# A new order of tasks in an attention and feed-forward kernel, half-array masks, and a cast on GpSimd

## The chip, the cores and the metric

The kernel runs on one core of one Trainium2 chip. The metric is the device time in microseconds (us) of one execution. The engines are TensorE (PE in the profile, its weight loads PEld), VectorE (DVE), ScalarE (ACT), GpSimd (POOL) and SyncE (SP), which only issues DMAs. Each works through its own queue in order, and they meet at semaphores.

## What is computed

For eight sequences of 1024 tokens with 256 channels the reference does, cut to what matters:

```python
xn = layernorm(x)
q, k, v = split(xn @ W_attn + b_attn)            # 16 heads of 16
q, k = rope(q), rope(k)       # its position index runs over the heads' axis
att = where(causal, q @ k.T / sqrt(16), -inf)
s = softmax(att) @ v @ W_proj + b_proj
g = silu((silu(xn @ Wg.T) * (xn @ Wu.T)) @ Wd.T) # hidden size 768, int weights / 127
out = x + s * g
```

## The kernel before

**Batches, units, slots.** The work is cut into 8 batches. A batch has 4 units, each of 4 heads, and a unit has 12 steps: a step is one block of keys (128) against one chunk of queries (512). `BLOCKS` lists the steps, and `width(n)` is the number of queries that step n needs: 512, 384, 256, 128 for the first chunk, and five times 512, then 384, 256, 128 for the second. So a batch has 48 slots, numbered 0 to 47, and slot s is step s mod 12 of unit s div 12. `body` runs over the slots, the first batch as "first", the last as "last", the six between as "mid".

**A slot on TensorE.** It has two halves. Each half begins with two score matmuls (`scores`, L672), which write keys by queries into a ring of three banks `st`. Each uses one half of the array's rows: 48 rows of split q and k and 2 rows that subtract the row maximum. Then come matmuls of the maxima (`maxima`, L696): q by k once more for the unit that is 16 slots ahead, also in pairs on the two halves of the rows, written into the ring of four banks `ring`. The maxima of the first half of a slot are on the diagonal, so a mask is added there: a matmul of `tri` with `identb` (L704) per bank, with all 128 rows. After that the first half has the slot's tasks, and the second half has the values (L722), the products of the exponentials of the step before with v, in four column strips. The second half has maxima in 8 of 12 slots.

**The other engines.** ScalarE takes the exponential of each score bank (`exps`, L896), two a half, and copies or activates the results of the tasks in the order of the table. VectorE reduces each bank of the maxima (L1030) and does its parts of the tasks. GpSimd sets the masked part of the exponentials to zero with an affine select (`mask`, L1250) at the start of a slot whose step before was on the diagonal (steps 0 to 3 and 8 to 11), then its parts of the tasks. SyncE stores q and k to a scratch in HBM, loads them back as stacks (`load_stack`, L508), six DMAs for q and six for k per unit, and loads and stores x.

**Tasks.** `TASKS` names, for each slot, the tasks of its first half; `END_TASKS` replaces it in the last batch from a slot on. The names: LNS (layer norm statistics, VectorE), LNR (the chain for the reciprocal deviation, 14 small operations on GpSimd, L470 to L478), LNA (normalise one tile, GpSimd), TX (transpose of xn), QK and V (projections), XC (a copy of the second half of the tokens, GpSimd), UPG and UPU (gate and up products of one of six chunks of 128 hidden units), DN (down product of 128 tokens), YT (transpose of the attention's result, read by VectorE), FT and FP (transpose and projection of the output), MT (transpose of the maxima, copied by ScalarE at L964). FP of one batch, its last two DN and one YT are done in the next. LNS, LNR, LNA, TX and QK are for the next batch.

`LAG` says how many half slots after the task's slot an engine does its part. The feed-forward chunk goes UPG: ScalarE tanh, VectorE `ga`; UPU: ScalarE copy `ups`, GpSimd product `hf` (L1281); then HI on ScalarE: `hT` high part, the 16-bit rounding of `hf` (L915); then LO on GpSimd: `hT` low part, the difference (L1286).

**Before the first slot.** `prologue` prepares weights, the first batch's norm, q, k and v, and then does the maxima of the first 16 steps, which VectorE has to reduce. SyncE loads the q stacks of units 0 and 1, ScalarE issues the 12 DMAs of their k stacks ahead of its copies of the last four QK.

Of the kernel before, what the change touches and what calls it, by code (L numbers as in the profile page):

```python
# [26 lines left out]
BLOCKS = [(0, k) for k in range(4)] + [(1, k) for k in range(8)]  # L27
# [27 lines left out]
def full_item(s):  # L55
# [18 lines left out]
    12: [("UPG", 0, 3), ("UPU", 0, 3), ("XC", 1)],
    13: [("YT", 0, 0), ("UPG", 0, 4), ("LNA", 0)],
    14: [("UPU", 0, 4)],
    15: [("FT", 2), ("FT", 3)],
    16: [("UPG", 0, 5), ("UPU", 0, 5), ("LNA", 2)],
    17: [("YT", 0, 1), ("LNA", 6)],
    18: [("YT", 1, 0), ("LNA", 3)],  # L80
    19: [("LNA", 1)],
    20: [("TX", 1, 0), ("DN", 0, 0), ("LNA", 4), ("LNA", 5), ("LNA", 7)],
    21: [("MT", 2), ("TX", 1, 1)],
    22: [("TX", 0, 1), ("DN", 0, 1)],
    23: [("QK", 0, 0, 1), ("QK", 0, 1, 1)],
# [17 lines left out]
    41: [("YT", 2, 1), ("UPU", 1, 5)],
    42: [("YT", 3, 0), ("QK", 1, 0, 0)],
    44: [("QK", 1, 1, 1)],
    45: [("MT", 0)],
# [11 lines left out]
EPI = [("YT", 3, 1), ("FT", 2), ("FT", 3), ("FP", 2), ("FP", 3)]  # L118
END_TASKS = {
    29: [("UPG", 1, 0)],  # L120
    30: [("DN", 0, 3)],
    31: [("UPU", 1, 0)],
    32: [("UPG", 1, 1)],
    33: [("MT", 3), ("UPG", 1, 2), ("UPU", 1, 1)],
    34: [("UPU", 1, 2)],
    35: [("UPG", 1, 3), ("UPU", 1, 3)],
    36: [("YT", 1, 1), ("UPG", 1, 4), ("UPU", 1, 4)],
    37: [("YT", 2, 0), ("UPG", 1, 5), ("UPU", 1, 5)],
    41: [("YT", 2, 1), ("DN", 1, 0)],
    42: [("YT", 3, 0), ("DN", 1, 1)],  # L130
    43: [("FT", 0, "end"), ("FT", 1, "end"), ("DN", 1, 2, "end")],
    44: [("FP", 0, "end")],
    45: [("DN", 1, 3, "end"), ("FP", 1, "end")],
# [13 lines left out]
def tasks_at(kind, slot):  # L147
    tasks = END_TASKS if kind == "last" and slot >= min(END_TASKS) else TASKS
# [4 lines left out]
def has_max(kind, slot):  # L153
# [152 lines left out]
def build_program(nc, x, w_attn, b_attn, w_proj, b_proj, w_gate_t, w_up_t, w_down_t, rope_cos, rope_sin, out):  # L306
# [8 lines left out]
    with ExitStack() as ctx:  # L315
# [18 lines left out]
        identb = sb("identb", [P, P], bf16)  # L334
# [87 lines left out]
        tri_done = sem("tri_done")  # L422
        pv_done = sem("pv_done")
# [106 lines left out]
        def _(sp):  # L530
# [42 lines left out]
            def task(kind, i, t):  # L573
                if t[0] == "QK":
                    _, hf_, which, c = t
                    if t == [u for u in BY["QK"].seen[kind] if u[1:3] == (hf_, which)][-1]:
                        store_parts(kind, i, hf_, which)
                        if hf_ == 0 and which == 1:
# [4 lines left out]
                if t[0] == "FP":  # L583
                    store_out(kind, i, t)
                    if t[1] < 2:
                        load_xo(own_batch(i, t), t[1] + 2)

            def prologue():
# [11 lines left out]

                sp.wait_ge(b_turned, 1)
# [18 lines left out]
            def body(kind, i):  # L620
                for slot in range(SLOTS):
                    for half in range(2):
# [29 lines left out]
        def _(pe):  # L652
# [22 lines left out]
            def maxima(kind, i, slot, half):  # L675
# [730 lines left out]
```

## Time and profile before

| | us |
|---|---|
| median of 3 runs | 1412.45 |
| lowest, highest | 1411.94, 1413.13 |
| the profiled execution | 1412.94 |
| its span, first to last instruction | 1411.2 |
| mean granted TensorE clock | 0.979 |

A profile shows one execution. Busy time of an engine is the union of its instructions' times; a matmul's time holds its way through the array, so two that overlap in the pipeline count once, and how far apart they start tells more than how long each lasts. The timeline merges instructions of one kind that follow each other and gives the count behind an x; in square brackets it gives the idle time before them and what ended it.

### The profile page before, as it was taken

The numbers are of one execution on the slowest core, as the hardware profiler recorded it, in microseconds if no ns is written. First come the engines' busy times: TensorE is split into PE (matmuls) and PEld (weight loads), VectorE is DVE, ScalarE is ACT, GpSimd is POOL, SyncE is SP. The second block draws the span as 40 slices with busy tenths as digits, with TensorE's granted clock in tenths as the row PEclk, the third lists the DMA queues.
The fourth block names the chain that finished last, engine by engine and source line by source line (L and its number), as shares of the span: only waits on it lengthen the run. The fifth ranks groups of instructions, "written<-read, shape, count | busy, mean of one in ns | idle before, by whom it ended". The sixth has DMA issues, their size and how long they took to land.

```text
span 1411.2 us, 28890 instructions
## 1 busy us (share of the span) xinstructions
PE 1333.2 (94%) x10631; PEld 549.7 (39%) x10631; DVE 1007.6 (71%) x1930; ACT 983.3 (70%) x2186; POOL 626.5 (44%) x751
## 2 busy tenths in 40 slices
PE   3899999999999999999999999999999999999986
PEld 1223433434344433434334343443334443343333
DVE  6688777777777767787777777777777777767711
ACT  2157677786767777676777767777776777778673
POOL 4117332573426444464435734265343643344352
PEclk9679999999999999999999999999999999999998
DMA  2620112202041020401213020410204002120101
GB/s 79 171 76 2 48 30 96 56 1 92 2 120 32 2 91 17 128 10 36 57 53 99 2 79 14 120 33 2 91 16 121 17 10 83 37 85 2 31 2 46
DMA packets 56769, 73.58 MB, mean 52 GB/s; under 512 B 9010, under 2 KB 34994, under 8 KB 56628
## 3 DMA queue, kind: packets, MB, share of 16 engines
q1 hardware_dynamic: 56052, 70.95, 16.7%
q8 instruction: 84, 1.38, 0.4%
q10 hardware_dynamic: 576, 0.79, 0.3%
q14 instruction: 57, 0.47, 0.1%
HBM read 46.01 MB, written 25.17 MB: 50 GB/s over the span
## 4 chain that ended last, share of the span: by engine, by line
PE 71%; ACT 11%; DVE 9%; issue 4%; POOL 3%; DMA 1%; ACTq 0%; POOLq 0%; SPq 0%; DVEq 0%
PE ring L730 24%; PE acc L722 15%; PE st L672 11%; PE ring L696 7%; PE ring L704 5%; ACT pexp L896 4%; PE ring L817 4%; DVE mx_a L1030 3%; ACT th L942 2%; PE ring L792 2%; DVE ga L1092 1%; ACT mT L964 1%; ACT parts L932 1%; PE ring L826 1%; PE ring L807 1%
## 5 line engine op out<-in xcount | busy, mean ns | idle before, releaser
L896 ACT ACTIVATE pexp<-st 128x512 f32<-128x512 f32 (+3 forms) x1536 | 659.4, 494 | 82.5 <-PE st L672 78.6
L1030 DVE TENSOR_REDUCE mx_a<-ring 128x1 f32<-128x512 f32 (+3 forms) x896 | 534.5, 646 | 134.3 <-PE ring L704 74.8
L1250 POOL TENSOR_SCALAR_AFFINE_SELECT pexp<-pexp 128x512 f32<-128x512 f32 x256 | 162.5, 635 | 510.3 <-ACT pexp L896 510.3
L722 PE MATMUL acc<-pexp,v_pad 128*17 128x512 f32 (+3 forms) x3072 | 324.3, 494 | 15.6 <-POOL pexp L1250 12.4
L672 PE MATMUL st<-q_st,k_st 50*128 50x512 f16 (+3 forms) x1536 | 299.8, 335 | 17.6 <-ACT pexp L896 16.1
L696 PE MATMUL ring<-k_st,q_st 48*128 48x512 f16 (+3 forms) x1536 | 270.0, 333 | 9.7 <-DMA k_st<-parts_scratch 6.0
L1030 DVE TENSOR_REDUCE mx_b<-ring 128x1 f32<-128x384 f32 (+3 forms) x384 | 212.8, 596 | 53.2 <-PE ring L704 50.4
L672 PEld LDWEIGHTS st<-q_st,k_st 50*128 50x128 f16 x1536 | 85.0, 93 | 409.1 <-ACT pexp L896 268.3
L1281 POOL TENSOR_TENSOR hf<-ga,ups 128x512 f32<-128x512 f32 x96 | 121.8, 1269 | 68.6 <-ACT ups L947 57.1
L1286 POOL TENSOR_TENSOR hT<-hf,hT 128x512 f16<-128x512 f32 x96 | 111.0, 1157 | 91.3 <-ACT hT L915 91.3
L704 PE MATMUL ring<-tri,identb 128*128 128x128 bf16 (+1 forms) x768 | 126.1, 247 | 0.0
L1092 DVE SCALAR_TENSOR_TENSOR ga<-th,ring 128x512 f32<-128x512 f32 x96 | 66.0, 688 | 57.4 <-ACT th L942 57.2
L722 PEld LDWEIGHTS acc<-pexp,v_pad 128*17 128x17 f32 x3072 | 51.5, 95 | 131.0 <-issue 108.1
L696 PEld LDWEIGHTS ring<-k_st,q_st 48*128 48x128 f16 x1536 | 84.3, 96 | 41.5 <-DVE mx_a L1030 11.9
L730 PE MATMUL ring<-w_dn,hT 128*128 128x256 bf16 x768 | 95.8, 275 | 0.0
L1083 DVE SCALAR_TENSOR_TENSOR parts<-ring,b_qk,parts 128x512 f16<-128x512 f32 x64 | 47.8, 750 | 65.9 <-ACT parts L932 65.9
L730 PE MATMUL ring<-xh,w 128*128 128x512 f16 x256 | 86.5, 388 | 2.0 <-DVE xl L1076 1.9
L704 PEld LDWEIGHTS ring<-tri,identb 128*128 128x128 bf16 x768 | 44.0, 98 | 107.5 <-issue 101.3
L947 ACT ACTIVATE ups<-ring 128x512 f32<-128x512 f32 x96 | 57.4, 598 | 40.6 <-PE ring L730 39.9
L932 ACT ACTIVATE parts<-ring,b_qk 128x512 f16<-128x512 f32 x64 | 43.7, 687 | 57.9 <-PE ring L730 48.9
L942 ACT ACTIVATE th<-ring 128x512 f32<-128x512 f32 x96 | 57.8, 602 | 31.4 <-PE ring L730 29.7
L730 PEld LDWEIGHTS ring<-w_dn,hT 128*128 128x128 f16 x768 | 73.0, 99 | 10.7 <-DVE mx_a L1030 2.2
(113 smaller groups left out, 1554.3 us busy)
## 6 DMA issues: line engine op xcount, KB each, us to landing
parts_scratch<-parts SPq DMA_DIRECT2D x32, 512.0 KB, 2.8
q_st<-parts_scratch SPq DMA_DIRECT2D x192, 64.0 KB, 2.4
k_st<-parts_scratch SPq DMA_DIRECT2D x180, 64.0 KB, 2.2
xn<-in_x SPq DMA_DIRECT2D x8, 1024.0 KB, 5.9
xo<-in_x SPq DMA_DIRECT2D x32, 256.0 KB, 2.8
out<-xo SPq DMA_DIRECT2D x32, 256.0 KB, 2.2
q_st<-mT SPq DMA_DIRECT2D x128, 4.0 KB
pexp<-in_w_attn SPq DMA_DIRECT2D x1, 768.0 KB, 4.5
```

Source lines behind the costliest of these rows:

```text
L672: nc.tensor.matmul(st[:, (GH * n + 2 * p + a) % NST, 0:w], k_st[rows, g, p, kb * P:(kb + 1) * P], q_st[rows, g, p, q0:q0 + w], start=True, ...
L696: mm = nc.tensor.matmul(dst[:, k * w:(k + 1) * w], q_st[rows, g, p, t * P:(t + 1) * P], k_st[rows, g, p, k0:k0 + w], start=k == 0, stop=ha ...
L704: nc.tensor.matmul(ring[:, b, 0:n * w].rearrange("p (s w) -> p s w", s=n)[:, :, w - P:w], identb[:, :], tri[:, 0:n, :], start=False, stop= ...
L722: mm = nc.tensor.matmul(acc[32 * j:32 * j + D + 1, CH - w:CH], v_pad[:, kb, GH * g + j, :], pexp[:, GH * (n % NSET) + j, 0:w], start=kb == ...
L730: mm = nc.tensor.matmul(dst, left, right, start=k == 0, stop=k == len(pairs) - 1)
L896: nc.scalar.activation(pexp[:, GH * (n % NSET) + j, 0:w], st[:, (GH * n + j) % NST, 0:w], ACT.Exp, scale=1.0 / (QK_SCALE * np.sqrt(D))).th ...
L942: nc.scalar.activation(th[:, th_buffer(kind, t), :], src, ACT.Tanh, scale=0.5 * QSCALE)\
L1030: nc.vector.reduce_max(dst, ring[:, b, 0:len(heads) * w].rearrange("p (s w) -> p s w", w=w), AX.X)\
L1092: nc.vector.scalar_tensor_tensor(out=ga[:, t[2] % 2, :], in0=th[:, th_buffer(kind, t), :], scalar=1.0, in1=src, op0=ALU.add, op1=ALU.mult) ...
L1250: nc.gpsimd.affine_select(out=t, in_=t, compare_op=ALU.is_ge, fill=0.0, base=0, pattern=[[0, GH], [1, P]], channel_multiplier=-1).then_inc ...
L1281: nc.gpsimd.tensor_tensor(hf[:, u, :], ga[:, u, :], ups[:, u, :], ALU.mult).then_inc(h_full, 1)
L1286: nc.gpsimd.tensor_tensor(hT[:, 1, m, :], hf[:, m % 2, :], hT[:, 0, m, :], ALU.subtract)\
```

## The change

1. `TASKS` and `END_TASKS` are written anew. All tasks of before are there, in other slots. Slots 16, 36 and 40 of a middle batch now have no task on TensorE (before: 19 and 43). `END_TASKS` begins at slot 28.
2. The mask of the maxima is added in the two halves of the array's rows: per bank two matmuls of 64 rows, the first over all 128 keys, the second over the last 64. `tri` is copied once to the other 64 partitions by a DMA, and `ident64` takes the place of `identb`.
3. HI, the high part of h, moves from ScalarE to GpSimd.
4. Before the first slot ScalarE issues the k stack of unit 0 alone (6 DMAs). That of unit 1 is issued by SyncE, behind the q stacks.
5. `BLOCKS` is written out in the same order, `DIAG_ORDER` is the identity, and the counts and the start and stop flags that follow from them come to the same. SyncE issues the stack loads of the next batch after the last QK of its first half, whichever that is, and the last loads of x in the last batch after FP 3.

```diff
 TASKS = {
-    0: [("FT", 1), ("DN", 1, 2)],
+    0: [("DN", 1, 2)],
...
-    16: [("UPG", 0, 5), ("UPU", 0, 5), ("LNA", 2)],
+    16: [("LNA", 0), ("LNA", 7)],
...
 LAG = {
-    "scalar": {"TX": 0, "QK": 0, "UPG": 0, "UPU": 0, "V": 0, "DN": 0, "FT": 0, "FP": 0, "MT": 0, "HI": 3},
+    "scalar": {"TX": 0, "QK": 0, "UPG": 0, "UPU": 0, "V": 0, "DN": 0, "FT": 0, "FP": 0, "MT": 0},
...
-    "gpsimd": {"LNR": 0, "LNA": 1, "XC": 1, "UPU": 2, "LO": 4, "FP": 2, "FP_G": 3, "FP_X": 4},
+    "gpsimd": {"LNR": 0, "LNA": 1, "XC": 1, "UPU": 2, "HI": 3, "LO": 4, "FP": 2, "FP_G": 3, "FP_X": 4},
...
@@ SyncE, prologue
+                sp.wait_ge(const_ready, 7)
+                sp.dma_start(tri[64:P, :, :], tri[0:64, :, :]).then_inc(tri_in, 16)
...
                 for g in range(2):
                     load_stack(sp, sp_stand, 0, g, 0, 1)
+                load_stack(sp, sp_stand, 0, 1, 1, 1)
@@ TensorE, maxima
-                    for a in range(2):
-                        b = bank(kind, t_ring, a)
-                        nc.tensor.matmul(ring[:, b, 0:n * w].rearrange("p (s w) -> p s w", s=n)[:, :, w - P:w],
-                                         identb[:, :], tri[:, 0:n, :], start=False, stop=True)\
-                            .then_inc(ring_ready[b], 1)
+                    for h in range(2):
+                        keys = P - 64 * h
+                        for a in range(2):
+                            b = bank(kind, t_ring, a)
+                            rows = slice(SIDE * a, SIDE * a + 64)
+                            mm = nc.tensor.matmul(ring[:, b, 0:n * w].rearrange("p (s w) -> p s w", s=n)[:, :, w - keys:w],
+                                                  ident64[rows, h, :], tri[rows, 0:n, 0:keys], start=False, stop=h == 1)
+                            if h == 1:
+                                mm.then_inc(ring_ready[b], 1)
@@ ScalarE, task
-                if t[0] == "HI":
-                    _, c, m = t
-                    act.wait_ge(h_full, BY["UPU"].at(kind, i, ("UPU", c, m)))
-                    nc.scalar.activation(hT[:, 0, m, :], hf[:, m % 2, :], ACT.Copy).then_inc(h_high, 1)
-                    return
@@ ScalarE, prologue
-                        for g in range(2):
-                            load_stack(act, act_stand, 0, g, 1, 1)
+                        load_stack(act, act_stand, 0, 0, 1, 1)
@@ GpSimd, task
+                if t[0] == "HI":
+                    _, c, m = t
+                    pool.wait_ge(h_full, BY["UPU"].at(kind, i, ("UPU", c, m)))
+                    nc.gpsimd.tensor_copy(hT[:, 0, m, :], hf[:, m % 2, :]).then_inc(h_high, 1)
```

The tables hold these tasks of TensorE at the places that the prediction speaks of (a middle batch, before and then after): slot 0 FT, DN and then DN; slot 4 two UPG, then DN; slot 11 V, then UPG, UPU (and LNR, before in slot 10); slot 12 UPG, UPU, then V, V, YT; slot 16 UPG, UPU, then none; slot 21 MT, TX, then MT, YT; slot 24 TX, FP, then DN; slot 26 QK, then four QK and DN; slot 28 FP, then UPU, YT; slot 33 MT, UPG, then MT, YT; slot 36 YT, V, then none; slot 40 QK, UPG, then none; slot 45 MT, then MT, YT.

The order of TensorE's instructions in slot 16 of a middle batch, before. `st` are the scores, `ring<-k_st,q_st` the maxima, `ring<-tri,...` the mask, `w_ga` and `w_up` a task, `acc` the values:

```order
L672 MATMUL st<-q_st,k_st 128x512 x2
L696 MATMUL ring<-k_st,q_st 128x384 x2
L704 MATMUL ring<-tri,identb 128x128 x2
L730 MATMUL ring<-xh,w_ga 128x512
...
L730 MATMUL ring<-xl,w_up 128x512
L672 MATMUL st<-q_st,k_st 128x512 x2
L696 MATMUL ring<-k_st,q_st 128x512 x2
L722 MATMUL acc<-pexp,v_pad 17x128 x4
```

The same slot of the changed kernel:

```order
L679 MATMUL st<-q_st,k_st 128x512 x2
L703 MATMUL ring<-k_st,q_st 128x384 x2
L714 MATMUL ring<-tri,ident 128x128 x2
L714 MATMUL ring<-tri,ident 128x64 x2
L679 MATMUL st<-q_st,k_st 128x512 x2
L703 MATMUL ring<-k_st,q_st 128x512 x2
L733 MATMUL acc<-pexp,v_pad 17x128 x4
```

The mask has four matmuls, two of them 64 wide, and the gate and up products have left the slot.

GpSimd's queue of a middle batch around one chunk and the chain of LNR, before (`pexp<-pexp` is the mask of the exponentials):

```order
L1281 TENSOR_TENSOR hf<-ga,ups 128x512
L1250 AFFINE_SELECT pexp<-pexp 128x4x128
L1286 TENSOR_TENSOR hT<-hf,hT 128x512
L1250 AFFINE_SELECT pexp<-pexp 128x4x128
L470 TENSOR_SCALAR lne<-lnv 128x8
...
L478 TENSOR_TENSOR rstd<-rstd,lnt 128x8
L1250 AFFINE_SELECT pexp<-pexp 128x4x128
```

And in the changed kernel:

```order
L1287 TENSOR_TENSOR hf<-ga,ups 128x512
L1291 CAST hT<-hf 128x512
L1256 AFFINE_SELECT pexp<-pexp 128x4x128
L1296 TENSOR_TENSOR hT<-hf,hT 128x512
L1256 AFFINE_SELECT pexp<-pexp 128x4x128
L474 TENSOR_SCALAR lne<-lnv 128x8
...
L482 TENSOR_TENSOR rstd<-rstd,lnt 128x8
L1256 AFFINE_SELECT pexp<-pexp 128x4x128
```

The cast has joined the chunk's other two operations, and the chain is one slot later: the mask behind it is the one of step 11, no longer that of step 10.

## Rows read from the trace of the kernel before

**Rows 1.** The page, part 4: the chain by engine

```profile
PE 71%; ACT 11%; DVE 9%; issue 4%; POOL 3%; DMA 1%; ACTq 0%; POOLq 0%; SPq 0%; DVEq 0%
```

**Rows 2.** Windows, middle batch: length; busy PE, PEld, DVE, ACT, POOL; clock

```profile
573.00:739.00 166.00, 161.90 (x1330) 67.13 (x1330) 123.49 (x237) 122.08 (x273) 78.32 (x92) 1.00 0.18 53
```

**Rows 3.** Timeline of PE, slot 28 to 29: start us, us, what

```profile
673.55 0.38 PE L696 MATMUL ring<-k_st,q_st 48*128 48x512 f16 x2
673.86 0.41 PE L722 MATMUL acc<-pexp,v_pad 128*17 128x128 f32 x8
674.21 0.75 PE L672 MATMUL st<-q_st,k_st 50*128 50x512 f16 x2
674.57 0.55 PE L696 MATMUL ring<-k_st,q_st 48*128 48x384 f16 x2
675.05 0.28 PE L704 MATMUL ring<-tri,identb 128*128 128x128 bf16 x2
675.18 0.38 PE L730 MATMUL ring<-xh,w_ga 128*128 128x512 f16 x1
```

**Rows 4.** Timeline of PE, slot 43 to 44

```profile
723.62 0.29 PE L704 MATMUL ring<-tri,identb 128*128 128x128 bf16 x2
723.84 0.39 PE L672 MATMUL st<-q_st,k_st 50*128 50x512 f16 x1
724.57 0.39 PE L672 MATMUL st<-q_st,k_st 50*128 50x512 f16 x1 [0.35 <-ACT pexp L896]
...
726.10 0.28 PE L696 MATMUL ring<-k_st,q_st 48*128 48x128 f16 x4
726.31 0.39 PE L704 MATMUL ring<-tri,identb 128*128 128x256 bf16 x2
726.54 0.38 PE L730 MATMUL ring<-xh,w 128*128 128x512 f16 x1
```

**Rows 5.** Timeline of ACT, slot 28 to 29

```profile
673.43 0.60 ACT L958 ACTIVATE so<-ring 128x512 f32<-128x512 f32 x1 [1.19 <-PE ring L817]
673.92 2.06 ACT L896 ACTIVATE pexp<-st 128x512 f32<-128x512 f32 x4
```

**Rows 6.** Timeline of PE and ACT, slot 33 to 34

```profile
690.49 1.00 ACT L964 ACTIVATE mT<-ring 8x1024 f16<-8x1024 f16 x1
...
691.14 0.28 PE L672 MATMUL st<-q_st,k_st 50*128 50x256 f16 x1
...
691.91 0.28 PE L672 MATMUL st<-q_st,k_st 50*128 50x256 f16 x1 [0.49 <-ACT pexp L896]
```

**Rows 7.** Timeline of POOL and PE, slot 11

```profile
609.02 0.25 POOL L470 TENSOR_SCALAR lne<-lnv 128x8 f32<-128x8 f32 x1
...
613.33 0.38 PE L696 MATMUL ring<-k_st,q_st 48*128 48x512 f16 x2
...
614.23 0.63 POOL L1250 TENSOR_SCALAR_AFFINE_SELECT pexp<-pexp 128x512 f32<-128x512 f32 x1
...
614.91 0.63 PE L722 MATMUL acc<-pexp,v_pad 128*17 128x256 f32 x8 [1.20 <-POOL pexp L1250]
```

**Rows 8.** Groups by form: busy us, mean ns, idle before them

```profile
L1281 POOL TENSOR_TENSOR hf<-ga,ups 128x512 f32<-128x512 f32 x96 | 121.8, 1269 | 68.6 <-ACT ups L947 57.1 <-DVE mx_b L1030 7.4 <-DVE ga L1092 4.0
...
L1286 POOL TENSOR_TENSOR hT<-hf,hT 128x512 f16<-128x512 f32 x96 | 111.0, 1157 | 91.3 <-ACT hT L915 91.3
...
L915 ACT ACTIVATE hT<-hf 128x512 f16<-128x512 f32 x96 | 62.1, 647 | 15.6 <-POOL hf L1281 15.6
...
L1348 POOL CAST w_ga<-hT 128x1536 bf16<-128x1536 int32 x1 | 1.5, 1463 | 28.4 <-DMA hT<-in_w_gate_t 28.4
```

**Rows 9.** The chain from 42 us: start us, us, what

```profile
41.96 0.35 ACTq L508
...
47.64 0.70 ACT parts L932
...
51.09 10.89 DVE mx_a L1030 x20
```

More of the change, by code:

```diff
@@ L24 @@
 NEG = -3.0e38
-BLOCKS = [(0, k) for k in range(4)] + [(1, k) for k in range(8)]
+BLOCKS = [(0, 0), (0, 1), (0, 2), (0, 3), (1, 0), (1, 1), (1, 2), (1, 3), (1, 4), (1, 5), (1, 6), (1, 7)]
+DIAG_ORDER = (0, 1, 2, 3, 4, 5, 6, 7, 8, 9, 10, 11)
 def width(n):
@@ L41, in diag_item @@
 def diag_item(s):
+    s = DIAG_ORDER[s]
     if s in (0, 1):
@@ L103 @@
[L103 to L104 removed]
+    4: [("DN", 1, 3), ("XC", 0)],
+    5: [("LNS", 0), ("LNS", 1), ("UPU", 0, 0)],
+    6: [("FP", 1)],
+    7: [("V", 0, 1), ("LNS", 2), ("LNS", 3)],
+    8: [("UPU", 0, 1)],
+    9: [("MT", 1), ("YT", 3, 1)],
+    10: [("FT", 2)],
+    11: [("UPG", 0, 2), ("LNR",), ("UPU", 0, 2)],
+    12: [("V", 1, 0), ("V", 1, 1), ("YT", 0, 0)],
+    13: [("LNA", 2), ("UPG", 0, 3), ("UPG", 0, 4)],
+    14: [("FT", 3)],
+    15: [("LNA", 4), ("UPU", 0, 3)],
@@ new lines @@
+    16: [("LNA", 0), ("LNA", 7)],
+    17: [("UPG", 0, 5), ("UPU", 0, 4)],
+    18: [("XC", 1), ("UPU", 0, 5)],
+    19: [("YT", 1, 0), ("LNA", 1)],
+    20: [("UPG", 1, 0)],
[6 rows of a table added]
+    27: [("UPG", 1, 1), ("UPU", 1, 0)],
+    28: [("UPU", 1, 1), ("YT", 1, 1)],
+    29: [("FP", 3)],
+    30: [("UPG", 1, 2)],
+    31: [("QK", 1, 0, 0)],
+    32: [("UPG", 1, 3)],
+    33: [("MT", 3), ("YT", 2, 0)],
+    34: [("UPU", 1, 2)],
+    35: [("V", 0, 0)],
+    37: [("QK", 1, 1, 0)],
+    38: [("YT", 2, 1)],
+    39: [("UPG", 1, 4), ("UPU", 1, 3)],
@@ L118 @@
 EPI = [("YT", 3, 1), ("FT", 2), ("FT", 3), ("FP", 2), ("FP", 3)]
+END_FROM = 28
 END_TASKS = {
[L120 to L131, printed above, removed]
+    28: [("YT", 1, 1), ("UPU", 1, 1)],
+    29: [("FP", 3)],
+    30: [("UPG", 1, 2), ("UPU", 1, 2)],
+    31: [("UPG", 1, 3), ("UPU", 1, 3)],
+    32: [("UPG", 1, 4), ("UPU", 1, 4)],
+    33: [("MT", 3), ("YT", 2, 0), ("UPG", 1, 5)],
+    34: [("UPU", 1, 5)],
+    38: [("YT", 2, 1), ("DN", 1, 0)],
+    39: [("DN", 1, 1)],
+    40: [("DN", 1, 2, "end")],
+    41: [("DN", 1, 3, "end")],
+    42: [("YT", 3, 0)],
+    43: [("FT", 0, "end"), ("FT", 1, "end")],
     44: [("FP", 0, "end")],
-    45: [("DN", 1, 3, "end"), ("FP", 1, "end")],
+    45: [("FP", 1, "end")],
 }
@@ L147, in tasks_at @@
 def tasks_at(kind, slot):
-    tasks = END_TASKS if kind == "last" and slot >= min(END_TASKS) else TASKS
+    tasks = END_TASKS if kind == "last" and slot >= END_FROM else TASKS
     return [t for t in tasks.get(slot, [])
@@ L288, in diag_count @@
 def diag_count(N_unit, n):
-    return 2 * GH * N_unit + (n if n < 4 else n - 4) + 1
+    return 2 * GH * N_unit + sum(is_diag(m) for m in range(n + 1))
 def wait(eng, sem, count):
@@ L577, in task @@
                         store_parts(kind, i, hf_, which)
-                        if hf_ == 0 and which == 1:
+                        if hf_ == 0 and t == [u for u in BY["QK"].seen[kind] if u[1] == 0][-1]:
                             for g in range(2):
@@ L584, in task @@
                     store_out(kind, i, t)
+                    if kind == "last" and t == ("FP", 3):
+                        load_xo(i, 0)
+                        load_xo(i, 1)
                     if t[1] < 2:
```

71 lines of the change are left out of this document (22 added, 49 removed), and 6 rows, old and new, of the table TASKS.

## Prediction

> **What bounds the kernel now.** A busy TensorE is a modelled number, so I read the chain first [rows 1]: 71% of it is TensorE, 11% ScalarE, 9% VectorE, 3% GpSimd. The windows [rows 2] show one middle batch of 166 us (six are alike) at full granted clock, with the other three engines busy for 123 us of it or less. So TensorE bounds most of the time, and in the rest it waits a few tenths of a microsecond for an engine that is not full but late. The timelines of one batch show where.
>
> A slot is one step of attention with its tasks. Its first half ends with the tasks; the second half is scores, often maxima, and the values of the step before. The second score matmul of a half needs the bank that the first exponential of the half before frees. In [rows 3] the values before it are only 128 wide (0.35 us until the next scores), ScalarE has copied a 512-wide task result first and begins four exponentials only then [rows 5]; so the score matmul of 674.21 is followed by its partner at 674.57, 0.36 us late, and the maxima behind it stretch as well (674.57 to 675.05, 0.48, where 0.26 would do: 384 columns at 2.4 GHz, 0.01 of gap, and 0.09 as below). I call this a narrow wait. In this batch it stands behind all eight slots whose second half has 128-wide values (0, 4, 12, 16, 24, 28, 36, 40): six times at 0.36, once at 0.64 and once at 0.41, 3.2 us, with about 1.5 behind them in the maxima, 4.7 in all. In [rows 6] ScalarE copies the transposed maxima (1.00 us) ahead of the exponentials, and the partner of the matmul at 691.14 starts at 691.91: 0.76 late, twice a batch, and 0.29 once, 1.8 in all. In [rows 7] GpSimd runs the chain of rstd, 5.2 us of small operations, and the mask of the exponentials waits behind it until 614.23; the values start at 614.91, 1.27 us late (scores, maxima and the switch would have let them start at 613.64).
>
> **The masks of the maxima.** Before: per bank one 128-row matmul of 128 or 256 columns. From start to start, [rows 3] give 675.05 to 675.18, 0.12 us for two of 128, and [rows 4] 726.31 to 726.54, 0.23 for two of 256. After: two passes of 64 rows, 128 then 64 keys wide, the two halves of the array at once. Pairs in halves already stand in the trace: 0.31 us for a 512-wide pair of maxima with the change of layout behind it (673.55 to 673.86), of which 512 columns take 0.213, so that layout change costs 0.09; and four 128-wide ones in 0.21 (726.10 to 726.31) less the same 0.09, so 0.06 for a pair of 128. A pair costs columns over 2.4 GHz and some 0.01. Then a single-head mask goes from 0.122 to 0.066 + 0.040 = 0.106, and a two-head mask from 0.228 to 0.119 + 0.066 = 0.185. There are 32 and 16 of them a batch: 32 x 0.016 + 16 x 0.043 = **1.2 us**. Bounds: without any gap 1.7; if a 64-wide pair costs as much as a 128-wide one, 0.4.
>
> Layout changes: the masks now join the maxima, so the change comes behind the mask instead of ahead of it; the count is the same where a task follows. Where none does, two are saved, as the mask is followed by half-array scores (723.62 to 723.84 in [rows 4] is 0.12 of mask and 0.09 of change). The new table leaves three slots so (16, 36, 40): 3 x 2 x 0.09 = **0.5 us**.
>
> The Trainium skill ("TensorE: Matmul & The Clock Gate", section "Wait — 56ns, not 53.3ns?") says that without hardware decode each MATMUL spends about 62 ns in microcode, which is the bound for short ones. By that rule four instructions in place of two would cost 0.25 us a mask, and the edit would lose (rival b). The trace disagrees: four 128-wide matmuls start within 0.21 us less the layout change.
>
> **The table.** Of the eight narrow slots, 0, 4 and 24 now hold one DN, whose result is 256 wide: half a wait, 0.27 each. 12 and 28 end with a YT, which VectorE reads: none. 16, 36, 40 hold nothing for TensorE; there ScalarE's four 512-wide exponentials (0.48 apart in [rows 5], 1.9 us) outlast TensorE's 1.4 us, so 0.5 at least. Slot 43 of before is such a slot and waits 0.73 ([rows 4], 723.84 to 724.57). I take 0.65. Left: 0.8 + 2.0 = 2.8 of 4.7, gain **1.9 us** (0.7 to 3). Slots 21, 33 and 45 keep the maxima's transpose but get a YT behind it instead of work that ScalarE must copy; slot 9 has that pair already and waits nowhere over 0.1. Gain **1.6 us** (1.0 to 1.8). The rstd chain moves one slot later and its mask meets slot 12, where TensorE has two V and a YT before the values: after the chain's start GpSimd needs 5.2 + 0.6 us, TensorE has slot 11's 3.2 and slot 12's first half of some 3.8, by their columns at 2.4 GHz. Covered, **1.3 us**; if that cover failed it would be back.
>
> **High part of h.** It takes 96 x 647 ns off ScalarE [rows 8], some 0.5 us each in the queue, 6 us a batch. GpSimd gets it. It has no such cast; the nearest rows are a cast of 1536 elements in 1463 ns (0.95 ns each, so 0.49 us for 512) and, on the other side, its two-input operations at 1.27 us. I take 0.55, as it reads one input: 6.6 us a batch on an engine that is busy for 78 of 166 [rows 2]. GpSimd moreover sits idle for 91.3 us in total [rows 8] waiting for exactly this ScalarE result, and no longer does. What is behind it: its low part (so DN 0,0, three slots later: covered), and the next mask. On ScalarE each copy stood ahead of the next exponentials, so the waits of slots 7, 19 and 43 (0.73 at 43 in [rows 4], some 0.4 at the others) should shrink: **1.0 us** (0 to 3).
>
> The Trainium skill ("GPSIMD Engine Reference", section 3.1) gives 1.03 cycles an element for at most two operations, at 1.2 GHz, and some 156 ns of dispatch on the engine beside it: an estimate of 0.60 us. The sum would be the same.
>
> New waits: four QK of six 512-wide matmuls and a DN of twelve 256-wide ones stand in slot 26 (6.5 us at 2.4 GHz, with ScalarE and VectorE behind), and SP starts the stack loads at slot 27 as before. Allowance **-0.6 us** (0 to -2).
>
> Middle batch: 1.2 + 0.5 + 1.9 + 1.6 + 1.3 + 1.0 - 0.6 = 6.9 us. Seven batches, 48. The last has no maxima after slot 31 and already a table of its own: 4.
>
> **Start.** ScalarE issues 12 k loads at 0.47 us (41.96 to 47.64) before it copies four QK results, and VectorE's maxima, which fill the time to the first scores, begin at 51.09 [rows 9]. Six issues go to SP, behind its own twelve: 2.7 us earlier, if the first stack has landed. Take 2.7 (0 to 2.7). The constants need three more operations and one DMA in the first microseconds, when GpSimd waits for the statistics anyway: nothing.
>
> BLOCKS, DIAG_ORDER, the counts and start flags of the values say the same as before: nothing.
>
> Sum 48 + 4 + 3 = 55 us. The profiled execution took 1412.94 us (span 1411.2); the median is 0.5 below. 1413 - 55 = **1358 us**.
>
> **Rivals.** (a) *The waits only move*: a queue is late at another slot, and only masks, layout changes and the start count: 8 x 1.7 + 2.7 = 16, 1397 us. For it: VectorE and ScalarE are at 74%, and this table has pairs that I allow little for. Against: each wait named has its own cause, and none is a full engine. 14%. (b) *The halves do not overlap for the masks* or short ones have a floor near 0.06 each: 0.21 and 0.37 us for the two kinds; 32 x 0.09 + 16 x 0.14 = 5.2 a batch lost, 1.2 not gained: 8 x 6.4 = 51, 1409 at worst, 1400 by the floor. Against: the maxima's pairs. 6%. By the rule of the Trainium skill above it would be 0.25 a mask, 32 x 0.13 + 16 x 0.02 = 4.5 lost, and 1404. (c) *GpSimd becomes the bound* and it is slower: product, cast and low part in one queue are 3.0 us ahead of a mask. If the cast costs 1.27, it is 3.7, longer than a slot; then six chunks a batch that stand beside masks make the values late by some 1.3 to 1.6 us like the one in [rows 7]: 9.6 lost for 6.9 gained, 8 x 2.7 = 22, less the start's 3: 1432. It decides from about 1.2 us a chunk on. Against: the one-input rows. 6%. (d) *More goes*: the start's idle gap before the maxima, in which the granted clock fell to half, closes too, and ScalarE's relief ends most small waits: 12 a batch, 1413 - 95 = 1318 to 1335. 12%.
>
> My forecast has 60%, from 1338 to 1378; what lies between it and (a) the last 2%. The range, 1328 to 1399, takes in (a) and the top half of (d), and the bounds of the terms. A difference of 0.2%, 3 us, is about what a measurement of this kernel can tell. Faster: forecast, (a), (d), and most of (b): 0.91. Within 0.2%: the rim of (b), 0.02. Slower: (c) and what I do not see: 0.07.
>
> **What would show it.** Two pairs per mask, 0.11 and 0.19 us from the first to the next work less the layout change; no wait of the values in slot 11 or 12; the second score matmul of slots 12 and 28 on time; slots 16, 36, 40 waiting 0.5 to 0.8 for ScalarE; a cast near 0.55 us on GpSimd, no idle for hT there; middle batches near 159 us; maxima from 48.4 us on. Wrong: mask pairs at 0.2 us and over; values waiting for masks in many slots; a long wait in or behind slot 26.

## The result and the profile after

| | before | after |
|---|---|---|
| median time, us (4 runs each on the same chip) | 1412.44 | 1333.90 |
| lowest to highest, us | 1411.94 to 1413.13 | 1330.34 to 1334.66 |
| profiled execution: time, span, us | 1412.94, 1411.2 | 1334.66, 1332.8 |

The change takes 78.5 us off: after over before is 0.9438, with an interval of 0.9422 to 0.9453. The forecast had a gain of 55 us.

The page of the changed kernel, its parts 1 and 4 (the chain answers to [rows 1]):

```profile
PE 1278.7 (96%) x11399; PEld 572.6 (43%) x11399; DVE 986.3 (74%) x1930; ACT 948.3 (71%) x2090; POOL 687.3 (52%) x850
...
PE 90%; DVE 4%; ACT 3%; DMA 1%; POOL 1%; issue 1%; ACTq 0%; POOLq 0%; SPq 0%; DVEq 0%
```

TensorE was 71% of the chain and is 90%. VectorE and ScalarE held 20% of it as engines that were late, not full, and hold 7%.

Windows of the changed kernel: 40 us of the start, and one middle batch (length; busy PE, PEld, DVE, ACT, POOL; clock), to set beside [rows 2]:

```profile
40.00:80.00 40.00, 32.59 (x162) 11.28 (x162) 32.57 (x61) 4.52 (x7) 4.40 (x3) 0.57 0.47 132
...
543.00:699.00 156.00, 155.14 (x1430) 70.33 (x1428) 121.06 (x237) 118.10 (x261) 85.84 (x104) 1.00 0.19 56
```

From first exponentials to first exponentials a middle batch took 166.0 us and takes 155.67, 10.3 less (forecast: 6.9). TensorE is busy for all but 0.9 us of the window, at full granted clock, where 4.1 us were open before. (Busy time is modelled. By start-to-start distances, as counted below, waits take 11.3 us of a batch before and 3.5 after.) The first batch went from 159.1 to 151.6, the last with the end from 174.5 to 168.0, the stretch before the first exponentials from 80.5 to 78.2. So 6 x 10.3 + 7.5 + 6.5 + 2.3 = 78 us: the whole difference. The window of the start has a mean clock of 0.57, and before it was 0.60: nothing of the gain comes from the clock.

Groups of the changed kernel on GpSimd, by form (busy, mean ns, idle before them), beside [rows 8]:

```profile
L1296 POOL TENSOR_TENSOR hT<-hf,hT 128x512 f16<-128x512 f32 x96 | 111.3, 1160 | 3.8
...
L1291 POOL CAST hT<-hf 128x512 f16<-128x512 f32 x96 | 58.7, 611 | 6.3
```

The cast takes 611 ns (the forecast took 0.55 us; the estimate from the Trainium skill's "GPSIMD Engine Reference", section 3.1, was 0.60, and the trace agrees with it). The 91.3 us for which L1286 sat idle behind ScalarE's copy are gone, as the prediction said.

Timelines of TensorE in the changed kernel: a two-head mask with its maxima, the empty slot 16, slot 33 with the first half of slot 34, and slot 11 (start us, us, what):

```profile
548.15 0.28 PE L703 MATMUL ring<-k_st,q_st 48*128 48x128 f16 x4
548.26 0.33 PE L714 MATMUL ring<-tri,ident 64*128 64x256 bf16 x4
548.52 0.39 PE L741 MATMUL ring<-xh,w_ga 128*128 128x512 f16 x1
...
579.94 0.25 PE L714 MATMUL ring<-tri,ident 64*128 64x128 bf16 x4
580.12 0.28 PE L741 MATMUL ring<-w,xh 128*128 128x128 f16 x2
...
593.22 0.25 PE L714 MATMUL ring<-tri,ident 64*128 64x128 bf16 x4
593.30 0.38 PE L679 MATMUL st<-q_st,k_st 50*128 50x512 f16 x1
593.96 0.39 PE L679 MATMUL st<-q_st,k_st 50*128 50x512 f16 x1 [0.28 <-ACT pexp L908]
...
653.64 0.61 PE L837 MATMUL ring<-ident,mx_p 128*8 128x128 f16 x8
654.23 0.63 PE L803 MATMUL ring<-ident,yT 128*128 128x128 f32 x4
...
656.04 0.28 PE L679 MATMUL st<-q_st,k_st 50*128 50x256 f16 x2
656.16 0.33 PE L703 MATMUL ring<-k_st,q_st 48*128 48x384 f16 x2
...
578.62 0.38 PE L703 MATMUL ring<-k_st,q_st 48*128 48x512 f16 x2
578.93 0.62 PE L733 MATMUL acc<-pexp,v_pad 128*17 128x256 f32 x8
```

- A two-head mask with its maxima ahead and one layout change takes 0.37 us (548.15 to 548.52); before it was 0.44 (726.10 to 726.54 in [rows 4]). The mask itself is 0.167, not 0.185. A one-head mask with the change of layout behind it takes 0.18 (579.94 to 580.12), of which 0.087 are mask (forecast 0.106). In slot 16, where scores follow in the same layout, they start 0.08 behind the mask; in slot 43 of [rows 4] it was 0.22.
- Slot 16 has the wait that the forecast left in it: the second score matmul starts 0.66 behind the first, where 0.01 do. The forecast took 0.65.
- In slot 33 the transpose of the maxima stands ahead of a YT. The 256-wide pair of scores behind it (656.04) starts together and its maxima follow after 0.12; in [rows 6] the second of this pair was 0.76 late.
- In slot 11 the values start 0.31 behind the maxima of 578.62. In [rows 7] it was 1.58, with GpSimd named. No values of slot 12 wait either.

### The profile page after: what moved, and what is told of

The parts are those of the page before. It is cut to its first block, busy times and chain, and to the rows that moved or that the text cites. A ratio compares the mean times of both kernels' runs of the same rounds, so it can differ in the third digit from the quotient of the medians.

```text
span 1332.8 us, 30434 instructions
## 1 busy us (share of the span) xinstructions
PE 1278.7 (96%) x11399; PEld 572.6 (43%) x11399; DVE 986.3 (74%) x1930; ACT 948.3 (71%) x2090; POOL 687.3 (52%) x850
## 4 chain that ended last, share of the span: by engine, by line
PE 90%; DVE 4%; ACT 3%; DMA 1%; POOL 1%; issue 1%; ACTq 0%; POOLq 0%; SPq 0%; DVEq 0%
PE ring L741 30%; PE acc L733 22%; PE st L679 16%; PE ring L703 8%; PE ring L828 4%; PE ring L714 3%; PE ring L803 3%; DVE mx_a L1036 2%; ACT pexp L908 2%; PE ring L837 1%; PE ring L818 1%; PE ring L751 1%; DVE mx_b L1036 1%; DMA xn<-in_x 1%; DMA k_st<-parts_scratch 0%
## 5 line engine op out<-in xcount | busy, mean ns | idle before, releaser
L679 PE MATMUL st<-q_st,k_st 50*128 50x512 f16 (+3 forms) x1536 | 282.5, 334 | 8.8 <-ACT pexp L908 8.3
L703 PE MATMUL ring<-k_st,q_st 48*128 48x512 f16 (+3 forms) x1536 | 264.2, 332 | 8.0 <-DMA k_st<-parts_scratch 5.0
L1287 POOL TENSOR_TENSOR hf<-ga,ups 128x512 f32<-128x512 f32 x96 | 122.1, 1272 | 14.6 <-issue 10.4
L714 PE MATMUL ring<-tri,ident 64*128 64x128 bf16 (+2 forms) x1536 | 121.9, 219 | 0.0
L714 PEld LDWEIGHTS ring<-tri,ident 64*128 64x128 bf16 x1536 | 84.2, 96 | 41.5 <-issue 2.6
L703 PEld LDWEIGHTS ring<-k_st,q_st 48*128 48x128 f16 x1536 | 81.2, 96 | 30.2 <-DVE mx_a L1036 14.3
L741 PE MATMUL ring<-xh,w 128*128 128x512 f16 x256 | 83.6, 385 | 1.9 <-DVE xl L1082 1.9
L741 PE MATMUL ring<-xh,w_ga 128*128 128x512 f16 x192 | 74.2, 386 | 0.0
```

The costliest lines, as they stand in the source:

```text
L679: nc.tensor.matmul(st[:, (GH * n + 2 * p + a) % NST, 0:w], k_st[rows, g, p, kb * P:(kb + 1) * P], q_st[rows, g, p, q0:q0 + w], start=True, ...
L703: mm = nc.tensor.matmul(dst[:, k * w:(k + 1) * w], q_st[rows, g, p, t * P:(t + 1) * P], k_st[rows, g, p, k0:k0 + w], start=k == 0, stop=ha ...
L714: mm = nc.tensor.matmul(ring[:, b, 0:n * w].rearrange("p (s w) -> p s w", s=n)[:, :, w - keys:w], ident64[rows, h, :], tri[rows, 0:n, 0:ke ...
L741: mm = nc.tensor.matmul(dst, left, right, start=k == 0, stop=k == len(pairs) - 1)
L1287: nc.gpsimd.tensor_tensor(hf[:, u, :], ga[:, u, :], ups[:, u, :], ALU.mult).then_inc(h_full, 1)
```

## The experiments

All times are medians; the ratio is to the kernel before on the same chip. "Changed" is the changed kernel, 1333.9 us. Batches are middle batches of the profiled execution.

### The parts undone or done alone

**e1: the changed kernel with the old masks.**

```diff
-                    for h in range(2):
-                        keys = P - 64 * h
-                        for a in range(2):
-                            ...
-                                                  ident64[rows, h, :], tri[rows, 0:n, 0:keys], start=False, stop=h == 1)
+                    for a in range(2):
+                        nc.tensor.matmul(..., identb[:, :], tri[:, 0:n, :], start=False, stop=True)
```

> The changed kernel with the masks of the maxima as before (one 128-row matmul per bank), all else kept. Theory A (masks are paid on TensorE): start to start a one-head mask with its layout change costs 0.215 us before and 0.181 now, a two-head one 0.32 and 0.26, so 2.0 us a batch, and three slots without a task save 0.09 twice: 2.6 x 8 = 20 us slower than the changed kernel, about 1354 us. Theory B (TensorE has slack where the masks stand, the gain came from the order alone): within 5 us of 1334.

Measured 1349.29 us, 0.9558 (0.9544 to 0.9572): the masks are worth 15.4 us here. A batch is 157.77, so the masks and layout changes are worth 2.1 of the 10.3 us (forecast 1.2 + 0.5), which leaves 8.2 for waits, where the forecast had 5.2.

**e2: the changed kernel with the high part of h on ScalarE.**

```diff
-    "scalar": {..., "MT": 0},
+    "scalar": {..., "MT": 0, "HI": 3},
-                    nc.gpsimd.tensor_copy(hT[:, 0, m, :], hf[:, m % 2, :]).then_inc(h_high, 1)
+                    nc.scalar.activation(hT[:, 0, m, :], hf[:, m % 2, :], ACT.Copy).then_inc(h_high, 1)
```

> The changed kernel with the high part of h back on ScalarE. Theory A (the table's slots had been late because ScalarE copied in front of exponentials, of which this is 0.5 us in 12 slots a batch): 8 us slower, 1342. Theory B (the relief of ScalarE carries the gain, and the new table relies on it): 25 us slower or more, 1359 on. Theory C (off the path): within 3 us.

Measured 1342.29, 0.9509 (0.9495 to 0.9523): worth 8.4 us, as theory A had it. A batch is mostly 156.55, 0.9 more; 0.8 of it are waits in slots 19 to 21 (0.22, 0.25 and 0.35 us) that the changed kernel does not have.

**e3: the kernel before with the new masks alone.** (The edit of e1, the other way.)

> The kernel before with the half-array masks alone. Theory A: the same saving as in the changed kernel, as TensorE bounds there too: 2.1 + 0.4 us a batch, 1412 - 20 = 1392. Theory B: hidden behind waits for ScalarE and VectorE, of which that kernel has more: 1405 or above.

Measured 1407.35, 0.9969 (0.9957 to 0.9981): 5 us, where the same edit is worth 15 in the changed kernel. A batch loses 0.6 us. TensorE gets to the same banks earlier and waits there longer: the waits of a batch, counted as below, go from 11.3 to 12.3 us, and the chain gives TensorE 69%, VectorE 11% and ScalarE 11%, where [rows 1] have 71, 9 and 11.

**e4: the kernel before with the high part of h on GpSimd alone.** (The edit of e2, the other way.)

> The kernel before with the high part of h on GpSimd alone. Theory A: 1.0 us a batch, 1404. Theory B (carries the gain): 1387 or below. Theory C (GpSimd's masks come later in the old order, as in slot 11): no gain or slower, 1412 to 1420.

Measured 1408.58, 0.9973 (0.9964 to 0.9983): 4 us, 0.7 a batch. The wait of slot 43 falls from 0.73 to 0.35 us; those of slots 7 and 19 stay at 0.43 and 0.38.

**e5: all of the change but the tables**, which are those of the kernel before.

```diff
-    16: [("LNA", 0), ("LNA", 7)],
+    16: [("UPG", 0, 5), ("UPU", 0, 5), ("LNA", 2)],
-    26: [("QK", 0, 1, 0), ("QK", 0, 0, 1), ("QK", 0, 1, 1), ("QK", 0, 0, 0), ("DN", 0, 3)],
+    26: [("QK", 0, 1, 0)],
...
```

> The changed kernel with the tables of before (TASKS and END_TASKS), so masks, the cast on GpSimd and the start kept. Theory A (the parts add up): 5 us from the masks alone, 4 from the cast alone and 2 from the start give 1401, and the table is the other 67. Theory B (masks and cast help each other once both are there, the table matters less): 1390 or below.

Measured 1400.87, 0.9923 (0.9908 to 0.9937), a batch 164.45. Masks, cast and loads together are worth 10.8 us in the old table (the kernel before has 1411.67 on the same chip); from there to the changed kernel the new table is worth 67. Since masks and cast bring 5 and 4 in the old table and 15.4 and 8.4 in the new one, part of the 67 is what the table lets them keep. TensorE's maxima and mask in slot 24 of e5:

```profile
648.73 0.86 PE L703 MATMUL ring<-k_st,q_st 48*128 48x512 f16 x2
649.20 0.47 PE L714 MATMUL ring<-tri,ident 64*128 64x128 bf16 x4
```

The second of the two maxima matmuls is 0.47 us late, as in the kernel before; this is used in the account of the waits below.

### Places of the table

**e6: the chain of rstd back at slot 10.**

```diff
-    10: [("FT", 2)],
-    11: [("UPG", 0, 2), ("LNR",), ("UPU", 0, 2)],
+    10: [("FT", 2), ("LNR",)],
+    11: [("UPG", 0, 2), ("UPU", 0, 2)],
```

> The changed kernel with the rstd chain one slot earlier, at slot 10, as before. Theory A (a mask of the exponentials stands behind 5.2 us of small operations and the values wait for it): 1.3 to 1.5 us in slot 11 of seven batches, 9 to 11 us slower, 1344. Theory B (the GpSimd queue has slack there since it no longer waits for ScalarE): within 3 us of 1334.

Measured 1366.16, 0.9677 (0.966 to 0.9694): 32 us slower than changed, three times what A said. The timeline of TensorE and GpSimd in slots 10 and 11, and windows of 4 us, the first from the same place of the first middle batch:

```profile
587.42 0.25 POOL L474 TENSOR_SCALAR lne<-lnv 128x8 f32<-128x8 f32 x1
...
592.65 1.23 POOL L1256 TENSOR_SCALAR_AFFINE_SELECT pexp<-pexp 128x512 f32<-128x512 f32 x2
...
589.97 0.38 PE L703 MATMUL ring<-k_st,q_st 48*128 48x512 f16 x2
593.34 0.85 PE L733 MATMUL acc<-pexp,v_pad 128*17 128x256 f32 x8 [2.99 <-POOL pexp L1256]
```

```profile
272.00:276.00 4.00, 1.70 (x25) 0.96 (x26) 1.04 (x3) 0.65 (x2) 3.27 (x8) 1.00 0.00 0
...
588.00:592.00 4.00, 2.35 (x18) 0.81 (x12) 3.09 (x6) 1.96 (x6) 2.08 (x11) 1.00 0.02 4
592.00:596.00 4.00, 2.66 (x24) 1.32 (x25) 0.65 (x2) 1.08 (x2) 3.42 (x6) 0.70 0.00 0
596.00:600.00 4.00, 4.00 (x59) 3.38 (x57) 1.20 (x4) 1.47 (x3) 0.00 (x0) 0.87 0.00 0
```

The chain starts at 587.42 and holds the mask until 592.65; the values, 0.31 behind the maxima in the changed kernel, start 3.37 behind them. So the wait is 3.06 us and not the 1.27 of the kernel before: slot 10 holds only an FT now, and TensorE reaches these maxima 2.55 us behind the chain's start, where [rows 7] have 4.31. Behind the wait the granted clock falls: the next two windows have means of 0.70 and 0.87. So it is in five of the six middle batches, which take 160.3 us, 4.6 more than in the changed kernel. In the first the same wait passes at full clock (1.00 at 272 and behind), and this batch is 159.73 where the changed kernel has 156.67: 3.06 more, the wait alone. The other 1.5 us are the clock.

**e9: the transpose of the maxima behind the YT** in slots 9, 21, 33 and 45.

```diff
-    33: [("MT", 3), ("YT", 2, 0)],
+    33: [("YT", 2, 0), ("MT", 3)],
```

> The changed kernel with MT behind YT in place of ahead of it, in slots 9, 21, 33 and 45. Theory A (what ScalarE copies last decides when the exponentials of the second half begin): the 0.9 us copy stands right ahead of them, as in slot 45 of the kernel before, 0.3 us in four slots a batch, 9 us slower, 1343. Theory B (as in slots 21 and 33 before, where another copied task stood there too): 0.76 each, 24 us, 1358. Theory C (the order within a slot does not matter): 1334.

Measured 1340.26, 0.9485 (0.9471 to 0.9499): 6.4 us slower, 1.1 a batch. The timeline of TensorE in slot 33, to set beside slot 33 of the changed kernel:

```profile
654.16 0.61 PE L837 MATMUL ring<-ident,mx_p 128*8 128x128 f16 x8
654.71 0.34 PE L679 MATMUL st<-q_st,k_st 50*128 50x384 f16 x2
...
655.96 0.57 PE L679 MATMUL st<-q_st,k_st 50*128 50x256 f16 x2
656.25 0.44 PE L703 MATMUL ring<-k_st,q_st 48*128 48x384 f16 x2
```

ScalarE's copy now stands ahead of the exponentials, and the pair at 655.96 takes 0.29 until the maxima instead of 0.12; until the first task it is 0.29 more in all, in each of the four slots. So the order within the slot is worth that much, with the YT as the cover. Slots 21 and 33 of the kernel before lost 0.76, with another copied task behind the transpose; that this task made the rest is read from [rows 6] and was not tested alone.

**e11: the four QK at slots 24, 24, 25 and 26** instead of all in 26.

```diff
-    24: [("DN", 0, 1)],
-    25: [("DN", 0, 2)],
-    26: [("QK", 0, 1, 0), ("QK", 0, 0, 1), ("QK", 0, 1, 1), ("QK", 0, 0, 0), ("DN", 0, 3)],
+    24: [("DN", 0, 1), ("QK", 0, 0, 1), ("QK", 0, 1, 1)],
+    25: [("DN", 0, 2), ("QK", 0, 0, 0)],
+    26: [("QK", 0, 1, 0), ("DN", 0, 3)],
```

> The changed kernel with the four QK of slot 26 spread as in the kernel before: two to slot 24, one to 25, one left. Theory A (maxima wait for a bank behind VectorE's part of a QK, 0.47 and 0.36 us in the kernel before, once per place where the block stands): 0.5 us in two slots a batch, 8 us slower, 1342. Theory B (VectorE has slack enough there): within 3 us.

Measured 1348.47, 0.9541 (0.9527 to 0.9555): 14.6 us slower. The timeline of TensorE in slot 24, and windows from that place in two batches, the first around the wait and behind it, the second behind it:

```profile
628.87 0.38 PE L703 MATMUL ring<-k_st,q_st 48*128 48x512 f16 x1
630.60 0.39 PE L703 MATMUL ring<-k_st,q_st 48*128 48x512 f16 x1 [1.36 <-DVE g L1106]
```

```profile
628.00:632.00 4.00, 2.64 (x26) 0.90 (x24) 3.08 (x6) 2.38 (x6) 0.64 (x1) 1.00 0.00 0
632.00:636.00 4.00, 4.00 (x18) 2.12 (x16) 1.23 (x2) 1.06 (x3) 0.00 (x0) 0.57 0.00 0
...
791.00:795.00 4.00, 4.00 (x33) 1.93 (x29) 1.73 (x3) 2.40 (x6) 0.00 (x0) 1.00 0.01 4
```

The second maxima matmul is 1.73 us late: its bank is read by VectorE's part of g, which stands behind parts of QK. Five of six middle batches are 1.8 longer than in the changed kernel (four of them 157.5). The remaining one, the third, is 159.2: there the clock fell to 0.57 behind the same wait.

**e12: two UPU moved into empty slots** (UPU 0,4 from 17 to 16; UPU 1,4 from 41 to 40). **e8** moves them too, and the YT of slot 38 to 40 behind the second.

```diff
-    16: [("LNA", 0), ("LNA", 7)],
-    17: [("UPG", 0, 5), ("UPU", 0, 4)],
+    16: [("LNA", 0), ("LNA", 7), ("UPU", 0, 4)],
+    17: [("UPG", 0, 5)],
```

> The changed kernel with two of its three empty narrow slots filled: UPU 0,4 from slot 17 to 16, UPU 1,4 from 41 and YT 2,1 from 38 to 40 (38 is then empty). Theory A (an empty narrow slot waits 0.87 us for ScalarE's exponentials, one with a copied task 0.55, one that ends with a YT 0.19): 0.3 + 0.7 us less a batch, some 0.2 lost at slot 38, 6 us faster, 1328. Theory B (the wait only moves to the slot behind): within 3 us.

> The changed kernel with UPU 0,4 in slot 16 and UPU 1,4 in slot 40, YT 2,1 left in slot 38. The run with YT moved too had 0.36 at slot 16 (0.87 without), 0.19 at slot 40 and a new wait of 0.52 at slot 38. Theory A (the waits of the slots add): 2 x 0.5 us a batch, less 0.2 lost behind, 4 to 8 us faster than the changed kernel, 1328. Theory B (what is won there is waited for behind): within 2 us.

Measured: e8 1332.81, 0.9438 (0.9423 to 0.9453); e12 1330.88, 0.9418 (0.9404 to 0.9432). Batches are 155.44 and 155.45, 0.2 less. In e12 the late score matmul at slot 16 costs 0.36 us instead of 0.65, but the two layout changes of 0.09 each are back: 0.29 less 0.18 is 0.11 a slot, and that is what a batch shows for two. The expectations had 0.87 and 0.55, because they added 0.2 for the maxima behind a late score matmul; from the first score matmul to the values slot 16 takes 1.19 us where 0.54 do, so the loss is 0.65 in all. In e8 the slot that lost its YT waits 0.41 anew. e12 is the fastest kernel measured, 3 us under the changed one, but the intervals overlap: it is not shown to be faster.

### Two details

**e7: the mask's four matmuls bank by bank** instead of alternating between the halves of the array.

```diff
-                    for h in range(2):
-                        keys = P - 64 * h
-                        for a in range(2):
+                    for a in range(2):
+                        for h in range(2):
+                            keys = P - 64 * h
```

> The changed kernel with the same four mask matmuls in another order: both passes of one bank, then both of the other, in place of pass by pass over the two halves of the array. Theory A (each half works at its own pace, and only neighbours in the queue overlap): only one pass of four overlaps, 0.05 us more for a one-head mask and 0.1 for a two-head one, 3.2 us a batch, 1360. Theory B (nothing overlaps so): 5.2 a batch, 1375. Theory C (the queue lets the other half run ahead, or masks never overlapped): 1334.

Measured 1334.67, 0.9454 (0.9438 to 0.947), no difference, as theory C had it. The timeline of TensorE in e7, a two-head mask and a one-head mask whose second bank is late:

```profile
547.03 0.28 PE L703 MATMUL ring<-k_st,q_st 48*128 48x128 f16 x4
...
547.40 0.39 PE L741 MATMUL ring<-xh,w_ga 128*128 128x512 f16 x1
...
638.52 0.32 PE L703 MATMUL ring<-k_st,q_st 48*128 48x384 f16 x1
638.69 0.22 PE L714 MATMUL ring<-tri,ident 64*128 64x128 bf16 x1
638.71 0.33 PE L703 MATMUL ring<-k_st,q_st 48*128 48x384 f16 x1
638.75 0.38 PE L714 MATMUL ring<-tri,ident 64*128 64x64 bf16 x3
```

0.37 us from maxima to task, as with alternating order. At 638.69 the mask of one half starts before the maxima of the other half (638.71), which stand ahead of it in the program. The changed kernel has such places too (mask at 639.81, maxima at 639.84).

**e10: the six k loads of the start back on ScalarE's queue.**

```diff
-                load_stack(sp, sp_stand, 0, 1, 1, 1)
-                        load_stack(act, act_stand, 0, 0, 1, 1)
+                        for g in range(2):
+                            load_stack(act, act_stand, 0, g, 1, 1)
```

> The changed kernel with both k stacks of the start issued by ScalarE, as before. Theory A (they stand ahead of four copies on which VectorE's maxima wait): 2.5 us slower, 1336. Theory B (the first stack's landing decides): same within 1 us.

Measured 1334.31, 0.9448 (0.9432 to 0.9464), no difference. The chain of the changed kernel, then that of e10, from the stores of parts to the maxima:

```profile
37.12 3.63 DMA parts_scratch<-parts
...
43.11 4.62 DMA k_st<-parts_scratch
47.73 0.24 issue
...
48.70 10.98 DVE mx_a L1036 x20
```

```profile
35.81 3.07 DMA parts_scratch<-parts
...
44.67 0.69 ACT parts L938
45.39 2.73 DVE parts L1089 x4
48.12 10.88 DVE mx_a L1036 x20
```

In the changed kernel the landing of the first stack decides (47.73), in e10 the parts of ScalarE and VectorE; both let the maxima begin at 48 to 49. In e10 the chain ran 1.3 us ahead already at the stores, before the edit can matter: the 24 matmuls ahead of them took 5.35 us there and 6.77 in the changed kernel, so a microsecond at the start is variation between executions. From the stores to the maxima e10 takes 12.31 us and the changed kernel 11.58. Over all kept traces it is 12.3 to 12.9 (mean 12.6) in the four with these loads on ScalarE and 10.7 to 12.4 (mean 11.5) in the ten with them on SyncE. So the edit seems to bring about a microsecond at that place, which the whole time cannot show.

## Why the prediction was right and where it fell short

Direction and range were right: faster, and 1333.9 lies between 1328 and 1399. The likeliest case was not: 1358, with a band from 1338 to 1378. The gain was under-estimated by 23 us of 78, and the time lies in rival (d)'s band, but only in part for (d)'s reasons: most small waits did end, by the new table (e5) more than by ScalarE's relief (8.4 us, e2), and the start's gap did not close. That the time still fell into the range was in part luck: the term for the narrow slots, too high, made up for half of what the list of waits lacked. What a middle batch's 10.3 us are, beside the steps of the forecast:

| step | forecast | measured |
|---|---|---|
| masks and layout changes | 1.2 + 0.5 | 2.1 (e1) |
| narrow slots | 1.9 | 0.1 |
| transpose of the maxima | 1.6 | 1.8 |
| rstd chain and the mask of slot 11 | 1.3 | 1.27 |
| waits of slots 7, 19, 43 | 1.0 | 1.5 |
| new waits | -0.6 | 0 |
| other waits, most for VectorE's banks, not in the forecast | 0 | 3.0 |

The measured waits are distances from the first score matmul of a half slot to its first task or values, against the same widths where nothing is late, in one batch of each trace. They add up to 7.7 where e1 leaves 8.2; 0.5 us has no place in the list.

- **The step that failed is the list of waits.** The prediction named waits of 7.8 us (it counted them as 9.3, see the narrow slots) of the 11.3 that a batch has. More were on the path, most of them second maxima matmuls and transposes behind a bank that VectorE reads for QK, the gate or the maxima before. The largest is in slot 24 of the kernel before; its timeline, and from the view of the tile parts in slots 24 to 28 who waited for it (us, times):

```profile
655.99 0.86 PE L696 MATMUL ring<-k_st,q_st 48*128 48x512 f16 x2
656.78 0.29 PE L704 MATMUL ring<-tri,identb 128*128 128x128 bf16 x2
```

```profile
  PEld ring L696: 0.8, 2
```

  0.79 us for a pair that takes 0.31 with the layout change; the maxima of slots 24 and 27 waited 0.8 us for VectorE's and ScalarE's parts. Beside these, 0.40 in slot 15, 0.25 in the transposes behind slot 24's mask, 0.30 each in slots 14 and 41, 0.23 in slot 38, and 0.37 in slot 17 for yT. A further 0.42 in slot 27 has the same cause as slot 24. In the changed kernel none of these is over 0.1. e5 shows that they went with the new table and nothing else: with all of the change but the tables, the waits of slots 14, 15, 17, 24, 27, 38 and 41 add up to 3.0 us, and in the kernel before to 2.8. That the table moved the QK into slot 26 was in the prediction only as a risk. e11 puts them back among masked slots and a wait for VectorE returns, at 1.73 us, though for another bank and in the other half of the slot. Which of the moved tasks ended each of the other waits was not tested; the banks of the ring are dealt in turn, so a moved task also changes whose bank a maxima matmul waits for.
- **Masks and layout changes**: the mechanism held, the size was low. I had given each pair 0.01 us of gap beyond its columns; a one-head mask costs 0.087 where 192 columns at 2.4 GHz are 0.080. Rival (b) is out. The 62 ns for each short MATMUL of the Trainium skill ("TensorE: Matmul & The Clock Gate", section "Wait — 56ns, not 53.3ns?") would make 0.25 of each mask; the 0.087 for all four speaks against it here. That section ties it to hardware decode being off.
- **Narrow slots**: the step's term was too high by 1.8, as its "4.7 in all" counts a piece of 1.5 us twice. Slot 16 of the kernel before has the same widths as [rows 3] and nothing late:

```profile
628.46 0.39 PE L672 MATMUL st<-q_st,k_st 50*128 50x512 f16 x2
628.69 0.33 PE L696 MATMUL ring<-k_st,q_st 48*128 48x384 f16 x2
628.95 0.28 PE L704 MATMUL ring<-tri,identb 128*128 128x128 bf16 x2
629.07 0.38 PE L730 MATMUL ring<-xh,w_ga 128*128 128x512 f16 x1
```

  From scores to task it takes 0.61 us, and [rows 3] take 0.97 (674.21 to 675.18). The loss is 0.36, the lateness of the second score matmul, and the stretch of the maxima is part of it. So there were 3.2 us to win. In the changed kernel 3.1 are left: the empty slots cost 0.60 to 0.65 each, as forecast, and 0.10 behind them; 12 and 28, "none", still lose 0.19 each, and so do 0, 4 and 24, where 0.27 was taken.
- **Transpose of the maxima**: right in size; e9 shows the share that the YT behind it has, 1.1 us over four slots.
- **The rstd chain**: right in the changed kernel. e6 shows what the cover is worth. Its own expectation carried before's 1.27 us over into a table whose slot 10 is shorter, and was wrong by a factor of three.
- **The high part of h**: the cast and the vanished idle came as said, and rival (c) is out: GpSimd is busy for 86 of 156 us. e2 gives 8.4 us in all, A's 8. But of the 1.5 us of waits in slots 7, 19 and 43 the cast alone ends 0.4 (e4); the rest needed the new table as well.
- **New waits**: none in or behind slot 26.
- **Last batch**: 6.5 instead of 4. **Start**: "2.7 us, if the first stack has landed" was tied to ScalarE's issues. In the traces they are worth about one (e10), as the landing of the first stack then decides, and the total of e10 does not show them; the rest of the 2.3 was there at the stores already and is variation.
- Rival (a), the waits only move, is in large part what happens to each part alone (e3, e4). It does not happen with the new table.

Sum: 3.4 a middle batch too little, over six 20 us; the rest of the 23 is the first batch, the last and the start together.

## What to carry to other kernels

Where TensorE runs at 97% of a window and still holds only 71% of the chain, count every wait of its matmuls from start to start, over the whole half slot so that no piece counts twice, before costing a new order of the work, not only those that the slowest engine causes: here over a third of the waits that went were not on the list, most of them at a second engine's banks. A saving on the bounding engine is kept only where no wait for another follows in the same slot; the same mask edit gave 5 us in the old order and 15 in the new. And price a moved wait by the slot that it lands in: the same chain of small operations cost nothing, 1.3 or 3.1 us of TensorE by one slot's difference and by what else is in it.

## What was not expected of the hardware

- The two row halves of the array run ahead of each other. In e7 a matmul of one half started 0.02 us before one of the other half that is ahead of it in the program, and the order of queueing made no difference to the masks. The Trainium skill ("TensorEngine Tiling (Array Packing)", section "Key Properties") says that tiles work independently, which agrees; "PSUM — Partial Sum Buffer", section "Engine vs sequencer instructions", of the Trainium skill says that matmuls start in program order; across the halves this trace shows otherwise.
- After a wait of 3.06 us (e6) TensorE's granted clock fell in five middle batches of six, in the one shown to means of 0.70 and 0.87 in the next two stretches of 4 us, part of each at its lower level of 1.2 GHz, and cost half as much again. In the first middle batch the same wait passed at 1.00. After the wait of 1.73 us in e11 it fell in one middle batch of six (0.57) and stayed at 1.00 in the others. In the kernel before, with waits up to 1.27 us, and in the changed kernel, with waits up to 0.65, the middle batches show 1.00.
